# Attention in a decoder layer: the maxima are transposed four slots later, and the passes are written out instead of looped

## What is computed

```python
q, k, v = (proj(q_heads), proj(k_heads), proj(v_heads))       # [B, 16, S, 32]
scores = jnp.einsum('bhqd,bhkd->bhqk', q, k) * scale
scores = jnp.where(causal, -jnp.inf, scores)                  # self attention only
attn = jax.nn.softmax(scores, axis=-1)
out = jnp.einsum('bhqk,bhkd->bhqd', attn, v)
```

## Time and profile before

| | |
|---|---|
| time, median of 3 runs | 4899.39 us (4897.51 to 4901.42) |
| the profiled execution | 4905.71 us, its span 4904.1 us |
| self attention | about 383 to 1100 us |
| cross attention | about 1845 to 3720 us |
| busy share of the span | TensorE 89%, VectorE 62%, GpSimd 47%, ACT 45% |
| mean granted TensorE clock | 0.937 |

### The profile page before, as it was taken

The page is one execution under the profiler, slowest core; times in us unless marked ns, Lnnn a source line. Parts: engine busy times, 40 slices in busy tenths (PEclk is TensorE's granted clock), DMA queues, the critical chain, the costliest instruction groups (busy, mean ns, idle before and its releaser), DMA issues. The chain is left out here.

```text
span 4904.1 us, 74698 instructions
## 1 busy us (share of the span) xinstructions
PE 4388.1 (89%) x23024; PEld 2724.6 (56%) x23024; DVE 3038.8 (62%) x5530; ACT 2192.0 (45%) x4027; POOL 2321.7 (47%) x790
## 2 busy tenths in 40 slices
PE   7988999997889979999999999999996649898998
PEld 5864555546668854444444444444443427686776
DVE  4436776753633347777777777777772546676776
ACT  1213555551221105666656565556563115544554
POOL 0012333330000017888988888888894123433445
PEclk8987999998889978999999999999998869999999
DMA  4554443406455560222322222222202552322232
GB/s 143 183 164 104 105 106 89 91 16 233 169 178 175 176 159 4 53 58 58 67 53 63 53 63 57 55 53 55 53 6 99 195 181 89 97 95 92 94 108 99
DMA packets 328345, 488.99 MB, mean 100 GB/s; under 512 B 22440, under 2 KB 188328, under 8 KB 321832
## 3 DMA queue, kind: packets, MB, share of 16 engines
q1 hardware_dynamic: 318472, 468.01, 34.3%
q10 hardware_dynamic: 7232, 8.40, 0.6%
q0 software_dynamic: 2304, 8.39, 0.5%
HBM read 315.91 MB, written 168.82 MB: 99 GB/s over the span
## 5 line engine op out<-in xcount | busy, mean ns | idle before, releaser
L851 DVE TENSOR_REDUCE cross_neg_max<-cross_scores 128x1 f32<-128x512 f32 x2048 | 1261.8, 678 | 493.8 <-PE cross_scores L681 493.8
L642 POOL TENSOR_TENSOR cross_partial<-cross_partial,cross_probs 128x2048 f32<-128x2048 f32 x320 | 1464.2, 4576 | 60.6 <-ACT cross_probs L803 35.3
L803 ACT ACTIVATE cross_probs<-cross_shifted 128x512 f32<-128x512 f32 x2048 | 1105.5, 600 | 831.1 <-PE cross_shifted L693 811.0
L681 PE MATMUL cross_scores<-cross_k_stack,cross_q_stack 96*128 96x512 f32 x2048 | 880.4, 442 | 61.7 <-DMA cross_v<-v 32.7
L693 PE MATMUL cross_shifted<-cross_q_stack,cross_k_stack 98*128 98x512 f32 x2048 | 848.9, 421 | 21.3 <-issue 17.6
L693 PEld LDWEIGHTS cross_shifted<-cross_q_stack,cross_k_stack 98*128 98x128 f32 x2048 | 386.5, 190 | 392.6 <-issue 254.6
L681 PEld LDWEIGHTS cross_scores<-cross_k_stack,cross_q_stack 96*128 96x128 f32 x2048 | 397.2, 194 | 328.7 <-DVE cross_neg_max L851 251.0
L803 ACT ACTIVATE self_probs<-self_shifted 128x512 f32<-128x512 f32 (+3 forms) x768 | 359.5, 492 | 385.1 <-PE self_shifted L696 311.1
L851 DVE TENSOR_REDUCE self_neg_max<-self_scores 128x1 f32<-128x512 f32 (+3 forms) x768 | 386.1, 547 | 222.5 <-PE self_scores L684 181.9
L707 PE MATMUL cross_out<-cross_probs,cross_v 128*32 128x512 f32 x4096 | 515.8, 623 | 0.0
L1407 POOL TENSOR_TENSOR experts_v<-experts_u,experts_rows 128x512 f32<-128x512 f32 x128 | 165.2, 1290 | 478.3 <-ACT experts_u L1490 478.3
(11 more groups left out here) (208 smaller groups left out, 6666.7 us busy)
## 6 DMA issues: line engine op xcount, KB each, us to landing
cross_k_stack<-k_hi SPq DMA_DIRECT2D x32, 1024.0 KB, 19.7
experts_yt_hi<-y_hi SPq DMA_DIRECT2D x64, 512.0 KB, 3.9
experts_yt_lo<-y_lo SPq DMA_DIRECT2D x64, 512.0 KB, 4.9
self_q_stack<-q_hi SPq DMA_DIRECT2D x32, 512.0 KB, 7.0
self_k_stack<-k_hi SPq DMA_DIRECT2D x32, 512.0 KB, 14.6
out_a_in<-attn SPq DMA_DIRECT2D x16, 1024.0 KB, 9.7
x<-out_y SPq DMA_DIRECT2D x16, 1024.0 KB, 5.5
kv_x_in<-in_ctx SPq DMA_DIRECT2D x16, 1024.0 KB, 5.8
```

The source lines that it names most:

```text
L642: nc.gpsimd.tensor_tensor(total, total, own, ALU.add).then_inc(pool_added.sem, 1)
L681: mm = nc.tensor.matmul(scores[at][:, 0:width], q_st[0:96, w, h, q0:q0 + P], k_st[0:96, w, h, half * WIDE:half * WIDE + width], start=True ...
L803: nc.scalar.activation(probs[:, e % NE % PB, h, f:], shifted[n % SHIFTED][:, f:], ACT.Exp).then_inc(exped.sem, 1)
L851: nc.vector.tensor_reduce(neg_max[:, column(a), half:half + 1], scores[n % (SLOTS * ROUNDS) % AHEAD][:, 0:width], AX.X, ALU.max, negate=Tr ...
```

## The change

The turn comes four pieces later: after the last piece of a round come four pieces of the following one, then the transposition (`TURN_AT = 4`). VectorE's reduction to the minimum stays directly behind the last maximum of the round. `neg_max` is doubled, since pieces of the next round now write it before the turn. The function that gave the turn a step of its own is gone, so each step of the cross attention has four slots (the last has five). `LEAD` stays 16 in the cross attention and goes from 12 to 18 in the self attention. ACT's write and load follow the turn by one and two steps as before; `turn_step` goes from 12 to 13 in the cross attention and stays 8 in the self attention. `passes` no longer loops on the device: all passes are straight code.

```diff
-    TURN = NPIECE
+    TURN_AT = 4
     SLOTS = NPIECE + 1
-    LEAD = NPIECE // 4
+    LEAD = 18 if causal else 16
...
-        def done(m):
-            to = SLOTS * sum(weights[:m]) // sum(weights)
-            before = SLOTS * sum(weights[:max(m - 1, 0)]) // sum(weights)
-            return TURN - LEAD + 1 if before <= TURN - LEAD < to else to
-
+        done = lambda m: SLOTS * sum(weights[:m]) // sum(weights)
         return range(done(s), done(s + 1))
+
+    def slot(n):
+
+        q, at = n // SLOTS, n % SLOTS
+        if at == TURN_AT:
+            return n, q - 1, None
+        return n, q, at - (at > TURN_AT)
+
+    def turn_slot(q, more):
+
+        return (q + 1) * SLOTS + (TURN_AT if more or q + 1 < ROUNDS else 0)
...
-        neg_max = sb("neg_max", [P, COLS, HALVES])
+        neg_max = sb("neg_max", [P, 2, COLS, HALVES])
...
         def passes(eng, one_pass):
 
-            one_pass(0, True, True)
-            with eng.Fori(1, PASSES - 1) as it:
-                one_pass(it, False, True)
-            one_pass(PASSES - 1, False, False)
+            for it in range(PASSES):
+                one_pass(it, it == 0, it < PASSES - 1)
...
-            turn_step = next(s for s in range(NS) if any((LEAD + i) % SLOTS == TURN for i in pieces_at(s)))
-
-            def write_rows(it, q):
-                act.wait_ge(maxed.sem, maxed.at(it, SLOTS * q + SLOTS))
+            turn_step = next(s for s in range(NS) if SLOTS + TURN_AT - LEAD in pieces_at(s))
+
+            def write_rows(it, q, more):
+                act.wait_ge(maxed.sem, maxed.at(it, turn_slot(q, more) + 1))
...
-            def turn_rows(it, n):
-                q = n // SLOTS
-
-                dve.wait_ge(maxed.sem, maxed.at(it, n))
-                nc.vector.tensor_reduce(neg[:, 0:COLS], neg_max[:, :, :], AX.X, ALU.min).then_inc(least.sem, 1)
+                if a == NPIECE - 1:
+
+                    dve.wait_ge(maxed.sem, maxed.at(it, n + 1))
+                    nc.vector.tensor_reduce(neg[:, 0:COLS], neg_max[:, q % 2], AX.X, ALU.min).then_inc(least.sem, 1)
+
+            def turn_rows(it, n, q):
+                turned = scores[n % (SLOTS * ROUNDS) % AHEAD]
```

More of the change, by code:

```diff
@@ L569, in passes @@
         def passes(eng, one_pass):
-            one_pass(0, True, True)
-            with eng.Fori(1, PASSES - 1) as it:
-                one_pass(it, False, True)
-            one_pass(PASSES - 1, False, False)
+            for it in range(PASSES):
+                one_pass(it, it == 0, it < PASSES - 1)
         def stream(r, s, more):
             if r == -1:
-                return [n for n in range(SLOTS + LEAD)]
+                opening = [(n + 1, 0, n) for n in range(TURN_AT)]
+                return opening + [slot(n) for n in range(TURN_AT + 1, SLOTS + LEAD)]
             found = [SLOTS * (r + 1) + LEAD + i for i in pieces_at(s)]
-            return [n for n in found if more or n < SLOTS * ROUNDS]
+            if more:
+                return [slot(n) for n in found]
+            last = SLOTS * ROUNDS + TURN_AT
+            return [slot(n) for n in found if n < SLOTS * ROUNDS] + [(SLOTS * ROUNDS, ROUNDS - 1, None)] * (last in found)
         def load_heads(sp, bh, w):
@@ L627, in _ @@
             pool.wait_ge(filled.sem, 2)
-            pool.memset(neg_max[:, :, :], 3.0e38).then_inc(filled.sem, 1)
+            pool.memset(neg_max[:, :, :, :], 3.0e38).then_inc(filled.sem, 1)
             pool.wait_ge(filled.sem, 3)
@@ L662, in _, with score @@
             pv_done.give_credit(pe)
+            pe.sem_inc(scored.sem, 1)
             block_done.give_credit(pe)
             sum_done.give_credit(pe)
-            def score(it, n):
-                q, a = n // SLOTS, n % SLOTS
+            def score(it, item):
+                n, q, a = item
                 r = q % ROUNDS
                 pe.wait_ge(maxed.sem, maxed.at(it, user_before(n, SLOTS * ROUNDS, AHEAD) + 1))
-                if a == TURN:
+                if a is None:
                     pe.wait_ge(least.sem, least.at(it, q + 1))
@@ L805, in one_pass @@
                             if s == turn_step + 1:
-                                write_rows(it, r + 1)
+                                write_rows(it, r + 1, more)
                             if s == turn_step + 2:
@@ L841, in _, with max_piece @@
             maxed.give_credit(dve)
+            dve.sem_inc(maxed.sem, 1)
             rows_out.give_credit(dve)
[L844 to L847, removed]
+            def max_piece(it, item):
+                n, q, a = item
+                if a is None:
+                    turn_rows(it, n, q)
                     return
@@ L850, in max_piece @@
                 dve.wait_ge(scored.sem, scored.at(it, n + 1))
-                nc.vector.tensor_reduce(neg_max[:, column(a), half:half + 1], scores[n % (SLOTS * ROUNDS) % AHEAD][:, 0:width], AX.X, ALU.max,
+                nc.vector.tensor_reduce(neg_max[:, q % 2, column(a), half:half + 1], scores[n % (SLOTS * ROUNDS) % AHEAD][:, 0:width], AX.X, ALU.max,
                                         negate=True).then_inc(maxed.sem, 1)
-            def turn_rows(it, n):
-                q = n // SLOTS
-                dve.wait_ge(maxed.sem, maxed.at(it, n))
-                nc.vector.tensor_reduce(neg[:, 0:COLS], neg_max[:, :, :], AX.X, ALU.min).then_inc(least.sem, 1)
+                if a == NPIECE - 1:
[3 more added lines that the diff above has]
+                turned = scores[n % (SLOTS * ROUNDS) % AHEAD]
                 dve.wait_ge(scored.sem, scored.at(it, n + 1))
                 dve.wait_ge(rows_out.sem, rows_out.at(it, 2 * q))
-                nc.vector.tensor_copy(neg_rows[0:COLS, 0], scores[n % (SLOTS * ROUNDS) % AHEAD][0:COLS, 0:P]).then_inc(rows_hi.sem, 1)
+                nc.vector.tensor_copy(neg_rows[0:COLS, 0], turned[0:COLS, 0:P]).then_inc(rows_hi.sem, 1)
                 dve.wait_ge(rows_hi.sem, rows_hi.at(it, q + 1))
-                nc.vector.tensor_tensor(neg_rows[0:COLS, 1], scores[n % (SLOTS * ROUNDS) % AHEAD][0:COLS, 0:P], neg_rows[0:COLS, 0].bitcast(F32),
+                nc.vector.tensor_tensor(neg_rows[0:COLS, 1], turned[0:COLS, 0:P], neg_rows[0:COLS, 0].bitcast(F32),
                                         ALU.subtract).then_inc(maxed.sem, 1)
```

2 lines of the change are left out of this document (1 added, 1 removed).

## The result

The changed kernel takes **4791.62 us** (median of 4 runs, 4790.16 to 4793.58); the kernel before took 4899.02 us beside it (4 runs, 4897.51 to 4901.42). The ratio is 0.9781, 95% interval 0.9764 to 0.9798. The forecast was 4789 us.

What follows compares the result with a forecast made beforehand. Bound: TensorE's own work plus what VectorE holds up through three scores buffers. Gains and losses 63 + 16 + 30 + 5.5 + 4 - 8 = 110.5 us, off 4899.4, gave 4789 us; range 4772 to 4832.

Steps and rivals of the forecast that it cites:

- Turn, clock and stall in the cross attention: Cross attention: later transposition gains 63 us, no clock falls at turns 16, waiting for the rows loses 8.
- VectorE's spare 1.31 us: Cross attention, undisturbed pair of steps of 6.18 us: VectorE idles 1.31, where the reduction to the minimum fits.
- The clock: Cross attention turns: ten falls to 1.2 GHz, 1.6 us each, vanish with the idleness; 16 us, bounds 0 and 16.
- The loop: TensorE's branches back over passes: 6.0 us each, five in cross attention, 30 us; one in self attention, 5.5 us.
- The rows: Cross attention round starts: the later load of negated maxima stalls TensorE, 0.25 us in 31 rounds, a loss of 8.
- The rival that the wait moves to the rows: Cross attention round starts: load lands late, stall brings clock falls back; gain only 59 us, 4840 us; chance 12%.
- the stall at which the sign turns: Cross attention: waiting for the rows makes the change slower only from 3.8 us a round, (110.5 + 8)/31.
- Self attention: Self attention: half of TensorE's small waits at transposition and burst return, 4 us, bounds +8 and -6; branch 5.5 more.
- The opening's wait: Self attention opening: TensorE's 13.0 us wait for the rows counted as 0 change, bounds +2 and -2.

Runs made afterwards that it cites:

- straight_only: The kernel before with the passes written out as straight code and nothing else changed; 4866.69 us, ratio 0.9924 to the old kernel.
- load_late_1: The changed kernel with ACT's load of the rows after the second exponential instead of the first, cross attention only; 4848.43 us, ratio 0.9892.
- turn_only: The changed kernel with the loop over passes put back, so the later turn alone; 4831.23 us, ratio 0.985 to the old kernel.
- load_late_3: The changed kernel with ACT's load of the rows after the fourth exponential instead of the first, cross attention only; 4918.19 us, ratio 1.0031.
- rotate: The changed kernel with the scores buffers taken by a slot number that runs on over the passes; 4788.86 us, ratio 0.9768.
- turn2_write2: The changed kernel with TURN_AT = 2 and, in the cross attention, ACT's write and load after the third exponential of their steps; 4790.79 us, ratio 0.977.
- changed_again: The changed kernel run once more, unaltered, beside later variants on the same chip; 4792.88 us, ratio 0.9779 to the old kernel.

## Why the prediction was right

**Turn, clock and stall in the cross attention.** Predicted 63 + 16 - 8 = 71 us; the turn alone made the stage 69.4 us shorter. The pairs of steps came out at 6.19, 6.10 and 6.83 (in a round without a listed wait for the rows) for the 6.2, 6.2 and 6.8 that were written down: VectorE's spare 1.31 us did hold the minimum, and one slot's worth of cast and subtraction did stand in the place of a maximum. Steps 12 and 13 together went from 8.23 to 6.18 us, which is the 2.06 of the sum. A regular round went from 57.48 to 55.64, the stall included.

**The clock.** Its falls at the turns were ten in the old kernel and none in the changed one. That they cost 1.6 us each was my reading of the slow blocks; in `straight_only`, where the falls come regularly, the round with one takes 59.13 us and its neighbour 57.5, so 1.6. What sets how many there are I did not know and do not: ten before, eight in `straight_only`.

**The loop.** Predicted 30 + 5.5; the loop alone gave 32.1 in the cross attention and 7.0 in the self attention, 37 in the time. In the attentions of the changed kernel TensorE has no wait `issue`, so nothing that it waited for was fetched late. What the prediction did not look at are the other loops of the kernel, whose branches back on TensorE's queue take 0.21 us (last section): the price of 6.0 us belongs to the long bodies of the attentions' passes.

**The rows.** This is the term that was mis-sized. Against `straight_only`, in the 24 rounds that do not end a pass, step 15 is 0.39 us longer and steps 14 and 0 together are 0.25 shorter. In the seven that end a pass step 15 takes 3.18 us there already, with TensorE waiting for ACT, and 3.19 now. Over all 31 the three steps are 2.6 us longer, where I had 8. The wait is listed 16 times, not 31, with up to 0.7; six more such starts are put down to ACT, and the other nine waits are too short for the list. Over the rounds the first shifted score starts 2.36 to 2.88 us after the issue of the load, and TensorE's queue comes to it 2.3 us after the issue (2.18 in the prediction): the 2.5 that I took between the bounds 2.0 and 3.0 was right, and the steps around give back more of the stall than I gave them.

On this latency the Trainium skill (DMA: Bandwidth & Descriptors, Anatomy of one DMA, the SWDGE path) had about 2.0 us fixed, and by that figure there is no stall. The section is on transfers that GpSimd issues, while this load is issued by ACT, so the figure is not one of this path. The trace has 16 waits, with 2.63 us in the one shown, and the measurement decides.

**The rival that the wait moves to the rows** was closer than its 12% told. I argued that a gap shorter than 1 us leaves the clock alone; the changed kernel's waits of up to 0.7 us do, in 31 rounds. But `load_late_1` shows the falls at an average wait of 33.0 / 31 = 1.06 us, sixteen of them. The changed kernel keeps its gain by some 0.8 us on a DMA whose landing itself varies by 0.5, and which took 3.2 us once in `turn_only` and once in `load_late_1`. My price for that case, 4840 us, was near (4848), but by another sum: I had 17 for the wait and 16 for the clock, and the wait grew by 27 and the clock took up to 29. And the stall at which the sign turns was wrong: I had 3.8 us a round, from the gain divided by 31, without the clock. `load_late_3` is 0.3% slower than the old kernel with 2.25 us in the mean.

**Self attention.** The stage lost 9.4 us, where 5.5 + 4 were predicted. The two rounds with the branch were 47.1 and 45.3 us in the old kernel, among others of 43.33: 5.7 for the loop. The regular rounds went to 42.96, 0.37 x 13 = 4.8 for the turn; three wraps of the buffers took 1.0 of it back. The opening's wait is 12.0 us, was 13.0, but the first shifted score comes 0.9 later in the stage, and the first round is 0.6 longer. That the sum of 9.5 met 9.4 is in part luck. By the single edits the loop gave 7.0, not 5.5, and the turn 1.3 in `turn_only`, or 2.4 from `straight_only` to the changed kernel, not 4. What `LEAD = 18` does there by itself was not tested.

**What the sum lacked.** The wrap at the end of a pass: 5.7 us by `rotate`. In the old kernel this slot follows the turn, where TensorE stood anyway, so I had no row for it; it was to be had from the code, by dividing 260 by 3. The nearness of 4789 to 4791.6 thus holds errors that cancel: the wrap cost 5.7 more than my sum had, the stall 5.4 less. A difference of 3 us is also within what the profiled executions scatter: theirs is 115.6 us, that of the medians 107.4.

What stays open: why the falls of `straight_only` come in fixed rounds, and why the last round of several variants has two or three of them and that of the changed kernel none. These cost about 1 us of the stage. What blurs differences of a few us between the variants more are the stages that none of them touches, which differ by up to 7.7 us.

## What to carry to other kernels

When a wait in an in-order queue is filled with work from behind it, everything downstream of the awaited result moves as well: here the load's time before it was needed fell from over 6 us to 2.3, and 0.8 us less would have cost half of the gain. So write down the slack of each later step (the write behind VectorE in ACT's queue too), and move those steps within their queue by single instructions, as `turn2_write2` does. Price an idle gap on TensorE as itself plus the clock that may fall behind it. And a ring of buffers that is indexed anew in each pass has to divide the slots of the pass, or to run on.

## What was not expected of the hardware

- Idle stretches of TensorE and the clock behind them, at one place in each of 31 rounds: up to 0.7 us (changed kernel) and 1.0 (`changed_again`), no fall; about 1.4 us, ten (old kernel) and eight (`straight_only`); 1.06 us in the mean and up to 1.7 (`load_late_1`), sixteen; 69.9 / 31 = 2.25 in the mean and up to 2.7 (`load_late_3`), 28. So 1.06 gave more than 1.4 did. Within `load_late_1` a gap of 0.88 has a fall behind it and one of 1.18 has none, and in `load_late_3` three of 2.1 to 2.3 have none: the length of the gap alone does not decide it.
- A branch back on TensorE's queue in the loops over passes takes 3.3 to 4.1 us each time, one that falls through 83 ns; the same branches on the other engines take 40 to 74 ns. In all other loops of the kernel a branch back on TensorE's queue takes 0.21 to 0.24 us. Here are those of the experts, in the old kernel (count, ns min/median/max):

```profile
L1335 PEldq COMPARE_BRANCH  x20: 76/208/211, 4083.8 to 4817.7; - x20
```

What tells the two kinds apart in the trace is the length of the body: about 2900 records on TensorE's queue (weight loads, matmuls and sequencer instructions) in a pass of the cross attention, 145 to 948 in the loops with the short branches. No run varies this length by itself.
